# Cross-attention with split products on one core: the first batch taken out of the loop, its context loaded first in halves over two queues, the weights turned behind it

## What is computed

```python
B, C, CI, N = (16, 512, 256, 1024)
g_x = conv1x1(g_w, g_b, x_2).transpose(0, 2, 1)
theta_x = conv1x1(theta_w, theta_b, x).transpose(0, 2, 1)
phi_x = conv1x1(phi_w, phi_b, x_2)
W = jnp.einsum('bnc,bcm->bnm', theta_x, phi_x) / phi_x.shape[-1]
y = jnp.einsum('bnm,bmc->bnc', W, g_x).transpose(0, 2, 1)
wy = conv1x1(w_w, w_b, y)
inv_std = jax.lax.rsqrt(bn_var + EPS)
wy = bn_gamma * (wy - bn_mean) * inv_std + bn_beta
return wy + x
```

## Time and profile before

| | us |
|---|---|
| median of 3 launches (809.64 to 811.26) | 810.12 |
| the profiled launch, its time | 808.35 |
| the profiled launch, its span | 806.5 |
| PE busy (share of the span) | 778.9 (97%) |
| DVE busy | 529.1 (66%) |
| POOL busy | 535.9 (66%) |
| ACT busy | 304.4 (38%) |
| HBM read / written | 69.35 MB / 33.55 MB |

### The profile page before, as it was taken

The page is one execution under the profiler, slowest core; times in us unless marked ns, Lnnn a source line. Parts: engine busy times, 40 slices in busy tenths (PEclk is TensorE's granted clock), DMA queues, the critical chain, the costliest instruction groups (busy, mean ns, idle before and its releaser), DMA issues.

```text
span 806.5 us, 11687 instructions
## 1 busy us (share of the span) xinstructions
PE 778.9 (97%) x4045; PEld 664.8 (82%) x4045; DVE 529.1 (66%) x901; ACT 304.4 (38%) x508; POOL 535.9 (66%) x351
## 2 busy tenths in 40 slices
PE   4499999999999999999999999999999999999997
PEld 2388888888888888888888888888888888888885
DVE  3858485775848667484875848577584866758254
ACT  2545242533414353342434424243452435334121
POOL 0888577785757868575785857688575777857400
PEclk9799999999999999999999999999999999999999
DMA  8735517163360826427072541717345071640202
GB/s 217 205 107 104 210 28 216 69 172 140 79 233 1 210 101 156 156 62 249 1 208 104 121 191 42 229 41 182 130 95 217 19 212 81 161 152 1 105 1 104
DMA packets 53011, 103.10 MB, mean 128 GB/s; under 512 B 2410, under 2 KB 35844, under 8 KB 52996
## 3 DMA queue, kind: packets, MB, share of 16 engines
q1 hardware_dynamic: 52996, 102.91, 43.6%
HBM read 69.35 MB, written 33.55 MB: 128 GB/s over the span
## 4 chain that ended last, share of the span: by engine, by line
PE 95%; DVE 2%; DMA 2%; SPq 1%; issue 0%; DVEq 0%; ACT 0%
PE wbank L540 57%; PE gbank L540 36%; DMA ctx_sb<-in_ctx_dram 2%; PE wbank L659 1%; DVE ctxT_lo L422 1%; DVE ctxT L386 1%; DVE z_lo L432 0%; SPq L217 0%; SPq L208 0%; DVE wp_lo L439 0%; DVE x_sb L530 0%; DVE wt_lo L439 0%; DVEq L66 0%; ACT ctxT_hi L297 0%; DVE zb_row L435 0%
## 5 line engine op out<-in xcount | busy, mean ns | idle before, releaser
L264 POOL TENSOR_TENSOR ctxT_lo<-ctxT,ctxT_hi 128x512 fp32r<-128x512 f32 x120 | 162.7, 1356 | 195.8 <-ACT ctxT_hi L297 195.8
L272 POOL TENSOR_TENSOR ctx_sum<-ctx_sum,ctxT 128x512 f32<-128x512 f32 x112 | 171.8, 1534 | 0.9 <-POOL ctx_sum L267 0.2
L280 POOL TENSOR_TENSOR x_lo<-x_sb,x_hi 128x1024 fp32r<-128x1024 f32 x64 | 151.8, 2407 | 2.7 <-ACT x_hi L297 2.7
L297 ACT ACTIVATE mt<-wbank 128x512 fp32r<-128x512 f32 x64 | 38.3, 598 | 250.7 <-PE wbank L540 250.7
L454 DVE TENSOR_TENSOR stage<-gbank,mt 128x384 f32<-128x384 f32 x64 | 28.4, 485 | 145.9 <-PE gbank L540 145.9
L530 DVE SCALAR_TENSOR_TENSOR x_sb<-wbank,const,x_sb 128x512 f32<-128x512 f32 x112 | 79.1, 747 | 67.6 <-PE wbank L540 67.6
L540 PE MATMUL wbank<-ctxT_lo,ctxT_hi 128*128 128x512 f32 x512 | 118.7, 389 | 0.0
L297 ACT ACTIVATE ctxT_hi<-ctxT 128x512 fp32r<-128x512 f32 x128 | 79.3, 629 | 102.9 <-DVE ctxT L386 102.9
L540 PEld LDWEIGHTS wbank<-ctxT_lo,ctxT_hi 128*128 128x128 f32 x512 | 95.1, 188 | 18.7
L386 DVE STREAM_TRANSPOSE ctxT<-ctx_sb 128x512 f32<-128x512 f32 x128 | 81.7, 683 | 10.4 <-DMA ctx_sb<-in_ctx_dram 10.4
L540 PE MATMUL wbank<-x_hi,wt_hi 128*128 128x512 f32 x256 | 81.7, 400 | 0.0
(11 more groups left out here) (100 smaller groups left out, 1346.9 us busy)
## 6 DMA issues: line engine op xcount, KB each, us to landing
ctx_sb<-in_ctx_dram SPq DMA_DIRECT2D x64, 512.0 KB, 8.4
x_sb<-in_x_dram SPq DMA_DIRECT2D x16, 2048.0 KB, 7.8
out_dram<-x_sb SPq DMA_DIRECT2D x64, 512.0 KB, 2.6
x_sb<-in_L_xattn_w_w_dram SPq DMA_DIRECT2D x1, 512.0 KB, 3.8
x_sb<-in_L_xattn_g_w_dram SPq DMA_DIRECT2D x1, 512.0 KB, 3.6
phi_nat<-in_L_xattn_phi_w_dram SPq DMA_DIRECT2D x1, 512.0 KB, 13.0
stage<-in_L_xattn_theta_w_dram SPq DMA_DIRECT2D x1, 512.0 KB, 12.7
bp_row<-in_L_xattn_phi_b_dram SPq DMA_DIRECT2D x1, 128.0 KB, 11.7
```

The lines of the kernel that those rows point to most:

```text
L264: nc.gpsimd.tensor_tensor(ctxT_lo[:, c, :], src, f(ctxT_hi[:, c, :]), ALU.subtract).then_inc(ctxT_lo_made, 1)
L272: nc.gpsimd.tensor_tensor(ctx_sum[:, :], ctx_sum[:, :], src, ALU.add).then_inc(ctxT_used, 1)
L280: nc.gpsimd.tensor_tensor(x_lo[:, k, :], x_sb[par][:, k, :], f(x_hi[:, k, :]), ALU.subtract).then_inc(x_lo_made, 1)
L297: nc.scalar.activation(dst, src, ACT.Copy).then_inc(sem_, 1)
```

## The change

Batches 0 and 1 are written out in front of a loop that now holds six pairs; batch 0 has branches of its own (`first(b)`).

- Loads: the context of batch 0 comes first, in two halves of 128 columns of each row (`in_first[0]`, `in_first[1]`, four DMAs each). SP issues partitions 0 to 63 (parts 0 and 1), ACT partitions 64 to 127 on its own queue; each issues four of the eight vectors between the halves. Then SP issues `w_w`, `theta_w`, `phi_w`, `x` of batch 0, `g_w`, `bp_row`.
- S and M of batch 0 go chunk by chunk: four matmuls of S and four of M for chunk c, then chunk c + 1, with M in four banks at once (seven banks with S). Chunks 4 to 7 of the turned context lie in `x_sb[1]`, so no place has to come free.
- POOL makes `ctxT_lo` of batch 0 (before: DVE), then the sums, then two of the four `x_lo`; DVE makes the other two.
- ACT scales `w_w` in place (before: DVE). Behind M, PE turns `w_w`, `theta_w` and `phi_w`, turns M, multiplies Z and `zb`, and then starts `theta(0, ...)`. The column sums stand behind `theta(0, ...)`.
- ACT and DVE do the splits of weights, G, Z and x of batch 0 in one hand-written interleaving. DVE's transposes of batch 1's first chunks stand behind the low half of G.

The core of the diff:

```diff
+            load_first_ctx(sp, (0, 1), 0)
+            load_vectors(sp, range(0, 4))
+            load_first_ctx(sp, (0, 1), 1)
             sp.dma_start(w_nat, w_w.rearrange("(m p) c -> p m c", p=P)).then_inc(in_w1, 16)
...
-            load_ctx(0)
...
+        def load_first_ctx(eng, parts, half):
+            src = ctx_in[0].rearrange("(k q) (a n) -> a q k n", q=32, a=QT)
+            cols = slice(half * (QN // 2), (half + 1) * (QN // 2))
+            for a in parts:
+                eng.dma_start(ctx_sb[32 * a:32 * a + 32, :, cols], src[a][:, :, cols]).then_inc(in_first[half], 16)
...
-            prep_ctx(0, first=True)
-            prep_x(0, 0)
+            for c in range(CH):
+                pool.wait_ge(ctxT_hi_made, c + 1)
+                lo_part(0, c, first_lo)
+            for c in range(CH):
+                sum_up(0, c)
+            sum_rest(0)
+            for k in (2, 3):
+                pool.wait_ge(x_hi_made, k + 1)
+                nc.gpsimd.tensor_tensor(x_lo[:, k, :], x_sb[0][:, k, :], f(x_hi[:, k, :]),
+                                        ALU.subtract).then_inc(first_x_lo_pool, 1)
...
+            for i in range(len(PLAIN)):
+                gram_sum(0, i)
+            z_lo_part(0)
+            gram_lo_part(0, 0)
+            first_x_lo_part(0)
+            z_lo_part(1)
+            gram_lo_part(0, 1)
+            first_x_lo_part(1)
+            z_lo_part(2)
+            gram_lo_part(0, 2)
+            z_lo_part(3)
             dve.wait_ge(zb_done, 1)
...
+                if first(b):
+                    next_ctx()
+                    dve.wait_ge(in_bp, 16)
+                else:
+                    columns_of_s()
                 theta(0)
...
+                if first(b):
                     for c in range(CH):
+                        s_chunk(c)
+                        pe.wait_ge(first_lo, c + 1)
+                        for i in range(KC):
+                            ins = mm(FIRST_M_BANK[i][:, :], hi_of(c, i), ctxT_lo[:, c, :], c == 0, c == CH - 1)
...
+                        if k == 0 and m == 0 and first(b):
+                            pe.wait_ge(tp_taken, 4)
+                            pe.wait_ge(z_taken, 4)
```

More of the change, by code:

```diff
@@ L189, in gram_bank, with first @@
             return gbank[i][:, at:at + P]
+        def first(b):
+            return isinstance(b, int) and b == 0
         def batches(eng, body):
-            with_pairs = (B - 2) // 2
-            with eng.Fori(0, with_pairs) as t:
+            body(0, 0, 0, True, True)
+            body(1, 0, 1, True, True)
+            with eng.Fori(1, B // 2 - 1) as t:
                 body(2 * t, t, 0, True, True)
@@ new lines, in _, with first_x_hi, first_gram_hi @@
+            act.wait_ge(scale_made, 1)
+            act.wait_ge(in_w1, 16)
+            for m in range(KC):
+                nc.scalar.activation(w_nat[:, m, :], w_nat[:, m, :], ACT.Identity,
+                                     scale=scale[:, m:m + 1]).then_inc(w_scaled, 1)
+            def first_x_hi(k):
+                hi(x_hi[:, k, :], x_sb[0][:, k, :], x_hi_made)
+            def first_gram_hi(i):
+                a, z = BANK_SPAN[i]
+                act.wait_ge(gram_f32, i + 1)
+                hi(gram_hi[:, a:z], stage[:, a:z], gram_hi_made)
@@ L380, in chain, with transpose_chunk @@
                 dve.wait_ge(vec_step, steps[0])
-            def transpose_chunk(b, c, free):
-                if free:
-                    dve.wait_ge(ctxT_used, CH * b + (c + 1 - RING))
-                nc.vector.transpose(ctxT[:, c % RING, :].rearrange("p (k q) -> p k q", q=32),
+            def transpose_chunk(b, c):
+                if not first(b):
+                    if isinstance(b, int) and b == 1 and c < RING:
+                        dve.wait_ge(ctxT_used, c + 1)
+                    else:
+                        dve.wait_ge(ctxT_used, CH * b + (c + 1 - RING))
+                nc.vector.transpose(turned_ctx(b, c).rearrange("p (k q) -> p k q", q=32),
@@ new lines, in z_lo_part @@
+            def z_lo_part(j):
+                dve.wait_ge(z_hi_made, j + 1)
+                nc.vector.tensor_tensor(z_lo[:, j, :], Z_BANK[j][:, :], f(z_hi[:, j, :]),
+                                        ALU.subtract).then_inc(z_taken, 1)
+            dve.wait_ge(w_turned, KI)
+            for k in range(KI):
+                nc.vector.tensor_copy(wsT[:, k, :], W_BANK[k][:, :]).then_inc(w_taken, 1)
+            for g, (dh, dl) in enumerate(((wt_hi[:, 0:2, :], wt_lo[:, 0:2, :]), (wt_hi[:, 2:4, :], wt_lo[:, 2:4, :]),
+                                          (wp_hi[:, 0:2, :], wp_lo[:, 0:2, :]), (wp_hi[:, 2:4, :], wp_lo[:, 2:4, :]))):
+                dve.wait_ge(tp_hi_made, g + 1)
+                nc.vector.tensor_tensor(dl, TP_BANK[g][:, :].rearrange("p (k c) -> p k c", k=2), f(dh),
+                                        ALU.subtract).then_inc(tp_taken, 1)
@@ L458, in body @@
[L458 to L461 removed]
+                        transpose_chunk(b + 1, c)
+                if not first(b):
+                    if nxt:
+                        next_ctx()
+                    for i in range(len(PLAIN)):
+                        gram_sum(b, i)
+                    for i in range(len(BANK_SPAN)):
+                        gram_lo_part(b, i)
@@ L577, in _ @@
[L577 to L579 removed]
+            turn_vectors()
             pe.wait_ge(ident_r_made, 1)
@@ L614, in turned, with column_sums @@
+                def column_sums():
+                    pe.wait_ge(sum_split, 2 * b + 2)
+                    mm(S_BANK[:, :], ones_r[:, :], sum_hi[:, :], True, False)
+                    mm(S_BANK[:, :], ones_r[:, :], sum_lo[:, :], False, True).then_inc(s_done, 1)
+                if first(b):
+                    turn_w()
+                    turn_theta_phi()
+                else:
+                    pe.wait_ge(work_free, NO * b + (3 - NO))
+                    column_sums()
                 def turned(blocks):
```

387 lines of the change are left out of this document (225 added, 162 removed).

## The result

| | before | after |
|---|---|---|
| median, lowest and highest of 4 launches, us | 810.21 (809.64 to 811.26) | 802.11 (801.54 to 803.79) |
| the profiled launch: time / span, us | 808.35 / 806.5 | 801.54 / 799.8 |
| batch 1 begins on PE, us | 85.82 | 80.28 |

The ratio is 0.9902 (95% interval 0.9884 to 0.9920): 6.5 to 9.4 us less. The forecast was 803.9 us in a range of 796.0 to 808.5, with batch 1 at 79.5.

What follows compares the result with a forecast made beforehand. Before batch 1, the chain of context DMA, DVE splits and late PE start bounds, with DVE the new bound; afterwards PE alone. Batch 1 moves from 85.8 to 79.5, 6.3 us less: 803.9 us from median 810.12, range 796.0 to 808.5.

Steps and rivals of the forecast that it cites:

- Step 1: Load of the context's first half: 1.05 MB at 350 GB/s from two queues, landed at 5.8 us.
- Step 2: First high part: a transpose and an ACT copy, ACT free at about 7.1 us; ready at 7.8 (7.2 to 9.7).
- Step 3: S and M on PE: 12.1 us plus 2.3 for a lower starting clock, M ending at 22.5 us (E).
- 4: PE done with Z and `zb`: Weight turns, M's transposes, Z and `zb` on PE behind M: done at E + 12.4, 34.9 us.
- Step 5: DVE, slowed by POOL, is the new bound: last `z_lo` at E + 18.4, 40.9 us; PE waits 6.0 us.
- Step 6: Theta to T: 6.6 us plus 2.1 for a fallen clock, T at 49.6; 1.8 us stall for DVE, ending at 55.7.
- Step 7: From the fourth T block to batch 1: 23.8 us as before, batch 1 beginning at 79.5.
- rival 3: Context load: second queue brings nothing, 205 GB/s, half lands at 7.9, batch 1 at 81.0, 805.4 us; chance 0.08.
- the tail: After batch 1 begins: 15 batches of 47.7 us and the end, unchanged.
- Rival 1: Ahead of theta: DVE keeps up, PE waits 1.4 us, batch 1 at 72.1, 796.4 us; chance 0.25.
- Rival 2: Context loads come late at 104 GB/s: E at 30.4, batch 1 at 87.4, 811.7 us; chance 0.09, in part or full.

Runs made afterwards that it cites:

- run 4: Changed kernel with all eight DMAs of the first context issued by SP, ACT issuing only its four vectors: 801.57 us.
- run 9: Changed kernel with SP holding back `w_w` and all later loads until the context's second half has landed: 804.13 us.
- run 1: Changed kernel with one added wait: POOL begins its two `x_lo` of batch 0 only after DVE has made its own two: 798.98 us.
- run 11: run 8 with the weight loads held back until the context's second half has landed: 795.87 us.
- run 12: run 8 with 62 extra narrow PE matmuls around the context's landing, and the first four chunks turned and rounded ahead of the vectors: 799.18 us.
- run 8: run 7 with POOL's two `x_lo` waiting for DVE's last `z_lo` instead of DVE's second `x_lo`: 794.62 us.
- run 3: Changed kernel with 24 unused matmuls of 512 columns filling PE's wait ahead of theta: 801.41 us.
- run 7: Changed kernel with POOL's `x_lo` behind DVE's, diagonals of S ahead of `th_lo`, DVE's transposes of batch 1 ahead of `low_lo`: 798.22 us.
- run 2: Changed kernel with DVE's four diagonals of the column sums in batch 0 moved ahead of theta's low parts: 800.38 us.
- run 5: Changed kernel with the first context loaded in whole 1 KB rows, SP to partitions 0 to 63, ACT to 64 to 127: 807.85 us.
- run 6: run 5 with SP on parts 0 and 2, ACT on 1 and 3, so both queues write the same half of the partitions: 809.17 us.
- run 10: Changed kernel with whole 1 KB context rows as in run 5, and SP's weight loads held back until all of it landed: 805.28 us.

## Why the prediction was right, step by step

| step | forecast | measured |
|---|---|---|
| 1: first half used | 5.8 | 7.37 |
| 2: first high part | 7.8 | 8.75 |
| 3: M ends (E) | 22.5 | 24.18 |
| 4: PE done with Z and `zb` | E + 12.4 | E + 12.3 |
| 5: last `z_lo`; PE's wait | E + 18.4; 6.0 | E + 18.0; 5.73 |
| 6: T begins; end of first L619 | 49.6; 55.7 | 50.55; 56.73 |
| 7: batch 1 | 79.5 | 80.28 |

**Step 1** was mis-sized. The forecast took the rate of `w_w` on the ground that its packets are as short as the context's. But halving the rows made them 512 B, and with these the rate is 211 to 249 GB/s, with one queue or two and with or without the weights beside them (runs 4, 9). This was rival 3's outcome (half at 7.9, batch 1 at 81.0), and the rival was too cheap at 0.08. The second queue did bring next to nothing (run 4), as it said, but what held the rate was the row of 512 B, which the rival did not name.

**Step 2** made up 0.6 of the 1.6 us lost: ACT's eight issues, its table load and its two small activations ended at 5.94, 1.2 ahead of the 7.1 assumed, so ACT was not waited for. The vectors (landed at 8.57) and the first high part (8.75) then came together.

**Step 3**: the slow start cost 3.0 us in this launch, not 2.3. That is M's end less the start of S less 12.2 us for eight chunks at 0.59 + 0.93. The same difference is 2.0 to 3.0 in the launches of runs 1 to 11, so the term had the right size and this launch lies at its upper end. The prediction calls it a lower clock, but the granted clock reads 1.00 all through it: the rows show only half the speed. Run 12 shows that narrow matmuls ahead do not shorten it.

**Step 5** carries the forecast, and its mechanism held (runs 1, 8). That its time fits to 0.4 us is in part luck, for errors cancelled in it. DVE's work alone takes 12.9 us from M's end (run 12), not 13.8. `gram_lo` 0, `gram_lo` 1 and `x_lo` 1 lost 0.3, 1.6 and 2.1 us to POOL (forecast 0.4, 2.0 and 2.4), while `x_lo` 0 lost 1.1 behind `sum_lo`, which the forecast had at nothing. POOL was busy to 39.3 (forecast: about 38).

**Step 6**: the low clock cost theta 1.64 us instead of 2.1 (run 3), and the wait for L619 was 1.75 instead of 1.8. The first of these varies too: behind a wait in which the clock fell, the same 12 matmuls took 4.41 to 5.46 us in the other runs. **Step 7** was 0.3 shorter than taken.

The sum: batch 1 came 0.8 us late, the tail was 1.1 us short, small terms gave 0.2, and the profiled launch lay 0.6 under its median, not 1.8. So it is 802.1 instead of 803.9. Two of the signs that the prediction names were missed narrowly: M ended at 24.18 (21 to 24 was said) and batch 1 began at 80.28 (79 to 80). Rival 1, DVE keeps up, did not come about by itself, but run 8 shows what it is worth when made to: its 796.4 was worked out with E at 22.5, and run 8 gave 794.6 with E at 23.11 and without the wait inside T. Rival 2 did not come about: chunk 4's high part was ready at 14.86, and PE came to that chunk at 18.10.

## What to carry to other kernels

When PE's start is moved forward, look for the next engine and set its operations beside those of its neighbour in time: here POOL's `x_lo`, wanted later, held up DVE's operations, wanted now, and run 8, with one wait and two moved calls, raised the gain over the kernel before from 8.1 to 15.2 us. Choose the event by the last operation that must go undisturbed: from run 7 to run 8 only that event moved, and the median fell by 3.6 us. Of the 3.85 us at batch 1, 1.7 are the shorter wait, 1.6 the clock that held behind it in that launch, and 0.6 an earlier end of M that the edit did not cause. Cutting a load in halves pays where it halves what must land first, even when the shorter rows slow it: whole rows were 5.7 us slower here, and still 3.2 with the weights held back (single launches).

## What the runs showed of the hardware

- The rate at which the context was loaded depended on the row and on the partitions together: 1 KB to both halves of the partitions 288 to 340 GB/s, 1 KB to one half 211 to 229, 512 B to both 220 to 249 (one queue: 211 to 215). From 2 to 4 us two queues moved 192 and then 345 GB/s, one queue 279 and then 226; why one microsecond differs so from the next is open.
- DVE's operations on 128x4 tiles take 0.16 to 0.18 us in the kernel before, where POOL is idle. Beside POOL they took up to 1.33 us, at 18 to 20 us. So the wait for POOL hits short operations with SBUF inputs as it does long ones. At 18 to 20 us it was hidden, but the one at 9.1 to 9.3 (0.84 to 0.99 us) lies on the chain of runs 1, 2 and 8, ahead of the low part of chunk 1.
- For the first 3 to 6 us of S and M the matmuls go at half their later speed, while the granted clock reads 1.00: that row does not show a slow start.
- Behind a wait of 1.7 to 1.8 us the clock fell in some launches (runs 3, 5, 6, 9) and in others not (the changed kernel, runs 1, 4, 10), with 1.5 us between them. Behind 2.2 to 2.3 us it held in run 8 and fell in run 11, again with 1.5 us between them. This is part of what launches of one kernel differ by, and it should be looked up before a difference of this size is put down to an edit.
